# Attention in a fused transformer block: heads one after another, two K/V/q slots, and exp in pieces of 1024 columns

## The reference

```python
xn = _layernorm(x)
x = x + attn(xn, W_qkv, b_qkv, W_out, b_out) + ffn(xn, gate_w, fc1_w, ..., alpha)
# attn
att = jnp.einsum('bhqd,bhkd->bhqk', q, k) * SCALE
att = jax.nn.softmax(jnp.where(causal, att, -jnp.inf), axis=-1)
out = jnp.einsum('bhqk,bhkd->bhqd', att, v)
# ffn: softmax gate, top 2 of 8 experts, gelu(x @ fc1) @ fc2, weighted sum
```

## Time and profile before

| | |
|---|---|
| median of the two runs | 7725.79 us (7260.15 and 8191.42) |
| profiled execution | 7260.15 us, span of its slowest core 7258.6 us |
| spans of all cores | 7247.8 to 7258.6 us, granted clock 0.871 to 0.873 |
| busy over the span | PE 79%, PEld 34%, DVE 20%, ACT 12%, POOL 8% |
| attention | 1166 to 2669 us |

### The profile page before, as it was taken

One profiled execution on the slowest core, in us unless ns is written; L12 is line 12 of the kernel. 1 busy time (PEld: TensorE's weight loads), 2 busy tenths in 40 slices (PEclk: granted clock), 3 DMA queues, 4 the chain that ended last, 5 costly groups with the idle time before them and its releaser, 6 DMA issues.

```text
span 7258.6 us, 69207 instructions; the slowest of 8 cores (7247.8 to 7258.6 us)
## 1 busy us (share of the span) xinstructions
PE 5759.5 (79%) x26321; PEld 2479.1 (34%) x26321; DVE 1438.2 (20%) x2612; ACT 855.4 (12%) x1651; POOL 554.2 (8%) x697
## 2 busy tenths in 40 slices
PE   2987882555555536659999999999699999999998
PEld 1432331222222212224444444444244444444443
DVE  5011003333333320001111111112112111111111
ACT  2100012233333320000000000000000000000000
POOL 0000000000000000000111111110011101110110
PEclk9988895666666667879999999999799999999999
DMA  3532402000000023374655556464765645555563
GB/s 100 70 53 41 79 32 76 24 24 24 24 23 24 15 51 95 95 157 59 72 68 70 70 61 79 59 81 50 162 79 59 82 58 71 69 71 69 61 79 81
DMA packets 737986, 474.56 MB, mean 65 GB/s; under 512 B 671984, under 2 KB 672128, under 8 KB 727424
## 3 DMA queue, kind: packets, MB, share of 16 engines
q0 software_dynamic: 642688, 310.67, 35.2%
q1 hardware_dynamic: 86000, 125.90, 5.8%
q10 hardware_dynamic: 8976, 33.56, 1.2%
HBM read 696.81 MB, written 75.50 MB: 106 GB/s over the span
## 4 chain that ended last, share of the span: by engine, by line
PE 76%; DVE 8%; issue 6%; DMA 4%; ACT 3%; another core or an unknown queue 1%; DVEq 1%; ACTq 0%; SPq 0%
PE psB L90 40%; PE psA L90 36%; DVE st L90 2%; ACT p_sb L90 2%; DVE p_sb L90 2%; DMA ct_sb<-ctxT_d 1%; DVE pT_sb L90 1%; DMA acc_sb<-out 1%; DVE o_sb L90 1%; DVE knm_sb L90 1%; DVE cte_sb L90 0%; ACT hT_sb L90 0%; DMA out<-acc_sb 0%; DVEq L89 0%
## 5 line engine op out<-in xcount | busy, mean ns | idle before, releaser
L90 PE MATMUL psA<-xnc_sb,f_sb 128*128 128x512 bf16 x8192 | 1816.4, 380 | 124.4 <-DMA acc_sb<-out 124.4
L90 PE MATMUL psB<-f_sb,hT_sb 128*128 128x512 bf16 x8192 | 1848.7, 384 | 47.3 <-ACT hT_sb L90 47.3
L90 DVE SCALAR_TENSOR_TENSOR acc_sb<-psB,comb_sb,acc_sb 128x1024 f32<-128x1024 f32 x512 | 657.3, 1284 | 3416.8 <-PE psB L90 3416.8
L90 PEld LDWEIGHTS psA<-xnc_sb,f_sb 128*128 128x128 bf16 x8192 | 782.7, 98 | 1139.8 <-issue 232.4
L90 PEld LDWEIGHTS psB<-f_sb,hT_sb 128*128 128x128 bf16 x8192 | 788.0, 99 | 1091.9 <-issue 209.0
L90 ACT ACTIVATE hT_sb<-psA 128x1024 bf16<-128x1024 f32 x256 | 262.4, 1025 | 3692.0 <-PE psA L90 3692.0
L90 POOL DMA_DIRECT2D f_sb<-fc_w x512 | 435.2, 861 | 3139.3 <-PE psB L90 1852.0
L90 PE MATMUL psB<-ident_sb,p_sb 128*128 128x128 bf16 x2176 | 306.0, 299 | 399.1 <-DVE p_sb L90 206.0
L90 ACT ACTIVATE p_sb<-psA,bnd_sb 128x512 bf16<-128x512 f32 (+3 forms) x640 | 400.2, 625 | 1061.3 <-PE psA L90 1011.8
L90 PE MATMUL psB<-pT_sb,vh_sb 128*128 128x512 bf16 (+3 forms) x640 | 225.8, 531 | 202.0 <-DVE p_sb L90 201.3
L90 PEld LDWEIGHTS psB<-ident_sb,p_sb 128*128 128x128 bf16 x2176 | 197.5, 129 | 509.5 <-issue 509.3
(11 more groups left out here) (93 smaller groups left out, 1894.8 us busy)
## 6 DMA issues: line engine op xcount, KB each, us to landing
f_sb<-fc_w POOLq DMA_DIRECT2D x512, 512.0 KB, 11.7
xt_sb<-x SPq DMA_DIRECT2D x16, 1024.0 KB, 5.0
wqk_sb<-w_qkv POOLq DMA_DIRECT2D x32, 512.0 KB, 10.0
x_sb<-x SPq DMA_DIRECT2D x16, 1024.0 KB, 9.1
out<-o_sb SPq DMA_DIRECT2D x16, 1024.0 KB, 5.1
acc_sb<-out SPq DMA_DIRECT2D x2, 8192.0 KB, 41.0
out<-acc_sb SPq DMA_DIRECT2D x2, 8192.0 KB, 27.7
qT_d<-ev_sb ACTq DMA_DIRECT2D x16, 512.0 KB, 7.6
```

The lines of the kernel that those rows point to most:

```text
L90: instr = getattr(engine, name)(*a, **kw)
```

## The change

It alters three things in stage 3.

1. The groups of a head run one after the other: (0,0), (0,1), (0,2), (0,3), (1,0), ... The bound of head h + 1 stands at the start of (h, 2); only head 0's stands ahead of the first group.
2. K, V and q have two slots each, and so has bnd_sb; the load of head h + 1 is listed at (h, 1). The columns for row sums are shared by blocks of the same parity.
3. Scores and exp work in pieces of 1024 keys: up to two matmuls of 512 (and the mask) fill half of psA, and one ACTIVATE reads it. psA is now two buffers, ps_P0 and ps_P1.

```diff
-        groups = []
-        for hp in range(0, n_h, 2):
-            for g in range(4):
-                groups.append((hp, g))
-                if hp + 1 < n_h:
-                    groups.append((hp + 1, g))
+        groups = [(h, g) for h in range(n_h) for g in range(4)]
...
-            ksl = h % 3
-            dk = (d_kA, d_kB, d_kC)[ksl]
+            ksl = h % 2
+            dk = d_kA if ksl == 0 else d_kB
...
-            if g == 1 and h % 2 == 0 and h + 2 < n_h:
-                kv_rdys[h + 2] = plan_kv_load(h + 2)
-                q_rdys[h + 2] = plan_q_load(h + 2)
+            if g == 1 and h + 1 < n_h:
+                kv_rdys[h + 1] = plan_kv_load(h + 1)
+                q_rdys[h + 1] = plan_q_load(h + 1)
...
                 plan_bnd(0)
-                if n_h > 1:
-                    plan_bnd(1)
-            if g == 2 and h % 2 == 0 and h + 2 < n_h:
-                plan_bnd(h + 2)
+            if g == 2 and h + 1 < n_h:
+                plan_bnd(h + 1)
...
-                lidx = (gi % 2) * 2 + (qbi % 2)
-                ab = 8 + 4 * lidx
-                P.guard_wait("scalar", f"lcols{lidx}")
-                for nb in range(nbs):
-                    n0 = nb * 512
-                    n1 = min(K, n0 + 512)
-                    bk = (bank_cur + nb) % 4
-                    b0 = bk * 512
+                ab = 8 + 4 * (qbi % 2)
+                nbs2 = (K + 1023) // 1024
+                P.guard_wait("scalar", f"lcols{qbi % 2}")
+                for nb in range(nbs2):
+                    n0 = nb * 1024
+                    n1 = min(K, n0 + 1024)
+                    pk = (bank_cur + nb) % 2
+                    b0 = pk * 1024
...
-                        i = t.matmul(ps_S[:, b0:b0 + (n1 - n0)],
-                                     qg[:, qbi * 128:(qbi + 1) * 128],
-                                     kth[:, n0:n1], start=True, stop=not diag)
+                        i = None
+                        for s0 in range(n0, n1, 512):
+                            s1 = min(n1, s0 + 512)
+                            i = t.matmul(ps_S[:, b0 + s0 - n0:b0 + s1 - n0],
+                                         qg[:, qbi * 128:(qbi + 1) * 128],
+                                         kth[:, s0:s1], start=True,
+                                         stop=not (diag and s1 == n1))
...
-                    P.set_guard(f"ps_S{bk}", se, se.n)
-                bank_cur = (bank_cur + nbs) % 4
+                    P.set_guard(f"ps_P{pk}", se, se.n)
+                bank_cur = (bank_cur + nbs2) % 2
...
-                    for nb in range(1, nbs):
+                    for nb in range(1, nbs2):
...
-            if g == 3 and h % 2 == 1 and h + 2 < n_h:
-                kv_rdys[h + 2] = plan_kv_load(h + 2)
-                q_rdys[h + 2] = plan_q_load(h + 2)
-                plan_bnd(h + 2)
```

More of the change, by code:

```diff
@@ L161, in build @@
         d_kB = Sem(ctx, nc, "d_kB")
-        d_kC = Sem(ctx, nc, "d_kC")
-        d_qC = Sem(ctx, nc, "d_qC")
         d_qA = Sem(ctx, nc, "d_qA")
@@ L598, in build @@
         a3 = ExitStack()
-        kt_sb = a3.enter_context(nc.sbuf_tensor("kt_sb", [128, 3 * S], BF16))
-        vh_sb = a3.enter_context(nc.sbuf_tensor("vh_sb", [128, 3 * S], BF16))
-        qh_sb = a3.enter_context(nc.sbuf_tensor("qh_sb", [128, 3 * S], BF16))
+        kt_sb = a3.enter_context(nc.sbuf_tensor("kt_sb", [128, 2 * S], BF16))
+        vh_sb = a3.enter_context(nc.sbuf_tensor("vh_sb", [128, 2 * S], BF16))
+        qh_sb = a3.enter_context(nc.sbuf_tensor("qh_sb", [128, 2 * S], BF16))
         p_sb = a3.enter_context(nc.sbuf_tensor("p_sb", [128, 8 * S], BF16))
@@ L604, in build @@
         cte_sb = a3.enter_context(nc.sbuf_tensor("cte_sb", [128, 2 * 512], BF16))
-        st3 = a3.enter_context(nc.sbuf_tensor("st3", [128, 28], F32))
+        st3 = a3.enter_context(nc.sbuf_tensor("st3", [128, 16], F32))
         q2_sb = a3.enter_context(nc.sbuf_tensor("q2_sb", [128, S], BF16))
-        bnd_sb = a3.enter_context(nc.sbuf_tensor("bnd_sb", [128, 4 * NT], F32))
+        bnd_sb = a3.enter_context(nc.sbuf_tensor("bnd_sb", [128, 2 * NT], F32))
         ps_S = psA
@@ L633, in plan_kv_load @@
         def plan_kv_load(h):
-            ksl = h % 3
-            dk = (d_kA, d_kB, d_kC)[ksl]
+            ksl = h % 2
+            dk = d_kA if ksl == 0 else d_kB
             kth = kt_sb[:, ksl * S:(ksl + 1) * S]
             vh = vh_sb[:, ksl * S:(ksl + 1) * S]
-            P.guard_wait("sync", f"kvh{ksl}")
+            P.guard_wait("sync", f"kv{ksl}")
             def s_kv(sy, h=h, kth=kth, vh=vh, dk=dk):
@@ L650, in plan_q_load @@
         def plan_q_load(hq):
-            qsl = hq % 3
-            dq = (d_qA, d_qB, d_qC)[qsl]
+            qsl = hq % 2
+            dq = d_qA if qsl == 0 else d_qB
             qh = qh_sb[:, qsl * S:(qsl + 1) * S]
-            P.guard_wait("sync", f"qh{qsl}")
+            P.guard_wait("sync", f"q{qsl}")
             def s_q(sy, hq=hq, qh=qh, dq=dq):
@@ L662, in plan_bnd @@
         def plan_bnd(hh):
[L663 to L666, removed]
+            hpar = hh % 2
+            dqh = d_qA if hpar == 0 else d_qB
+            qhf = qh_sb[:, hpar * S:(hpar + 1) * S]
             P.wait("vector", dqh, q_rdys[hh])
@@ L674, in plan_bnd @@
             P.wait("tensor", ve, q2_ve)
-            P.guard_wait("tensor", "ps_S0")
+            P.guard_wait("tensor", "ps_P0")
             def t_qn(t):
@@ L695, in plan_bnd @@
             bnd_ve = ve.n
-            P.set_guard("ps_S0", ve, bnd_ve)
+            P.set_guard("ps_P0", ve, bnd_ve)
             P.wait("scalar", ve, bnd_ve)
@@ L707, in build @@
             par = gi % 2
-            ksl = h % 3
-            dk = (d_kA, d_kB, d_kC)[ksl]
+            ksl = h % 2
+            dk = d_kA if ksl == 0 else d_kB
             vh = vh_sb[:, ksl * S:(ksl + 1) * S]
             kth = kt_sb[:, ksl * S:(ksl + 1) * S]
-            if g == 1 and h % 2 == 0 and h + 2 < n_h:
-                kv_rdys[h + 2] = plan_kv_load(h + 2)
-                q_rdys[h + 2] = plan_q_load(h + 2)
+            if g == 1 and h + 1 < n_h:
+                kv_rdys[h + 1] = plan_kv_load(h + 1)
+                q_rdys[h + 1] = plan_q_load(h + 1)
             kv_rdy = kv_rdys[h]
             q_rdy = q_rdys[h]
-            qsl = h % 3
-            dq = (d_qA, d_qB, d_qC)[qsl]
+            qsl = h % 2
+            dq = d_qA if qsl == 0 else d_qB
             qg = qh_sb[:, qsl * S + g * 512:qsl * S + (g + 1) * 512]
@@ L739, in build @@
                 P.wait("tensor", dk, kv_rdy)
[L741 to L748 removed]
+                ab = 8 + 4 * (qbi % 2)
[6 more added lines that the diff above has]
+                    b0 = pk * 1024
                     diag = (n1 == K)
[L750 removed]
+                    P.guard_wait("tensor", f"ps_P{pk}")
                     def t_s(t, qbi=qbi, qb=qb, n0=n0, n1=n1, b0=b0, qg=qg,
                             kth=kth, diag=diag):
[L754 to L756 removed]
+                        i = None
[5 more added lines that the diff above has]
+                                         stop=not (diag and s1 == n1))
                         if diag:
@@ L771, in sc_exp @@
                                           AF.Exp,
-                                          bias=bnd_sb[:, (h % 4) * NT + qb:
-                                                      (h % 4) * NT + qb + 1],
+                                          bias=bnd_sb[:, (h % 2) * NT + qb:
+                                                      (h % 2) * NT + qb + 1],
                                           scale=SCALE,
@@ L776, in build, with v_li, v_ps2 @@
                     P.on("scalar", sc_exp)
-                    P.set_guard(f"ps_S{bk}", se, se.n)
-                bank_cur = (bank_cur + nbs) % 4
+                    P.set_guard(f"ps_P{pk}", se, se.n)
+                bank_cur = (bank_cur + nbs2) % 2
+                if qbi == 3:
+                    P.set_guard(f"q{qsl}", pe, pe.n)
                 exp_se = se.n
                 if qbi == 3 and g == 3:
-                    P.set_guard(f"bndbuf{h % 4}", se, exp_se)
+                    P.set_guard(f"bndbuf{h % 2}", se, exp_se)
                 P.wait("vector", se, exp_se)
-                def v_li(vv, nbs=nbs, ab=ab, lidx=lidx):
+                def v_li(vv, nbs2=nbs2, ab=ab, qbi=qbi):
                     a = st3[:, ab:ab + 1]
-                    for nb in range(1, nbs):
+                    for nb in range(1, nbs2):
                         vv.tensor_add(a, a, st3[:, ab + nb:ab + nb + 1])
-                    i = vv.reciprocal(st3[:, 2 + lidx:3 + lidx], a)
+                    i = vv.reciprocal(st3[:, 2 + qbi % 2:3 + qbi % 2], a)
                 P.on("vector", v_li)
-                P.set_guard(f"lcols{lidx}", ve, ve.n)
+                P.set_guard(f"lcols{qbi % 2}", ve, ve.n)
                 P.wait("vector", ve, ve.n)
-                def v_ps2(vv, pq=pq, K=K, lidx=lidx):
+                def v_ps2(vv, pq=pq, K=K, qbi=qbi):
                     i = vv.tensor_scalar(pq[:, 0:K], pq[:, 0:K],
```

(4 more changed lines are left out.)

5 lines of the change are left out of this document (removed).

## The result

| | before | changed |
|---|---|---|
| median of all runs | 7581.59 us (13 runs) | 7428.57 us (14 runs) |
| lowest | 7259.7 us | 7135.42 us |
| ratio | | 0.9852, 95% interval 0.9806 to 0.9899 |
| core 0: span | 7258.0 us | 7125.5 us |

The changed kernel is 1.5% faster (1.0 to 1.9%), 124 us between the lowest runs; within 2%, as the likeliest case had it. The medians lie some 300 us above the lowest runs because in many executions of both kernels the cores of one or both dies show a lower granted clock for part of the time, so all that follows compares lowest runs, and of the traces the stretch of attention on cores where it was not so. From lowest to lowest run the ratio is 0.983; the 0.9852 also counts a run of 7202.51. The rows of the changed kernel are those of core 0.

What follows compares the result with a forecast made beforehand. It took attention to be bound by a circle of waits between TensorE, ScalarE and VectorE, with no engine full. Its terms, -3 - 5 - 107 = -115 us, taken from the profiled 7260, gave 7145 us, range 7080 to 7215.

Steps and rivals of the forecast that it cites:

- the likeliest case: Whole kernel: a measured time within 2% of the kernel before, chance 0.81.
- term 1: Attention, new order of groups: -0.41 us per head pair, -3 us in all.
- term 2: Start of attention: first scores wait for one bound, -6.9 us; head 1's bound costs 1.76 later; net -5 us.
- term 3: Attention, exp in pieces of 1024 columns: 6.7 us less per head, -107 us over 16 heads.
- The bound's credit: Attention groups holding a bound computation: it costs 1.76 us each, credited twice per head pair.
- rival A: Attention: TensorE's clock rises with shorter waits, -60 us more, 7085 us; chance 0.12.
- A stall from having two halves: Block 3 of g = 2 groups: exp waits about 0.1 us because only two PSUM buffers are left.
- rival B: Attention exp: a joining saves only 0.19 us on ScalarE, 48 us less gained, 7193 us; chance 0.07.
- At no cost: Loads of K, V and q with two slots add no time; without cover, up to 7 us a head.
- C: Attention: the order is not neutral, bounds hide less than credited, +25 us for term 1, 7173 us; chance 0.08.
- D: Attention: coarser hand-overs keep TensorE at 1.2 GHz, 184 to 361 us more, 7329 to 7506 us; chance 0.04.

Runs made afterwards that it cites:

- x9: Changed kernel with pieces of 512, four banks and four sets of sums put back, leaving the new order, two slots and later bound: 7232.14 us at the lowest.
- x3: Changed kernel with the removed row-sum adds put back as adds of a zero column: 7206.48 us.
- x4: Kernel before with exp that accumulates no row sum, the adds kept: 7200.37 us and 7200.74 us, ratio 0.9926.
- x2: Kernel before with only pieces of 1024, two PSUM halves and fewer row-sum adds: 7155.21 us, ratio 0.9886.

## Why the prediction was right or wrong

The mechanism was right in outline: the stage is a circle of waits, the wide exp brings most of the gain, and the stage lost what the sum had for it and some 12 us more. The stated time was not: the median over all runs is 7428.57 us, outside 7080 to 7215.

The step that failed is the base of the sum, "the trace is of the first and I forecast against it". 7145 is 115 us less than the one profiled execution, 7260.15. The median of the kernel before, over 13 runs, is 7581.59, and the changed kernel's lies 153 us below it. The median given already stood 466 us above the profiled run; I noted the distance without putting it into the range, and a forecast of a median over such executions had to reach up to them. Against the three lowest runs 7145 compares with 7135 to 7141 us.

Part of that closeness is luck, since two terms are off in opposite directions. "Measured" in this table is in means over the cores, for the sums of groups 1473.6 us before, 1452.0 in x9 and 1352.9 in the changed kernel.

| | predicted | measured |
|---|---|---|
| term 1, order of groups | -3 | -23 |
| term 2, start | -6.9, and +1.8 for the bound that moves | -6.6, and +1.7 |
| term 3, wide exp | -107 | -99 |
| sum, and time | -115, 7145 | -127 (attention), 7135 |

The lowest runs differ by 124 us; the rest is within what the cores differ by.

**Term 1: mis-sized, 3 for 23.** Taking the groups' durations from the kernel before assumed that a kind costs the same whatever stands two groups ahead. The bound's credit held (1.7 us). With the new order TensorE stays longer at its upper level, and the 63 groups became 22 us shorter where my sum had them 1 to 2 us shorter (-3, and 1.8 for the bound that moves in). This is rival A's mechanism at somewhat over a third of its size and in a place that I had not named: not shorter waits but other neighbours. The granted clock over the groups shows it, small as it is: 0.61 to 0.62 on the eight cores before, 0.64 on the eight of x9.

**Term 2: right.** From the first bound to the first score matmul 5.9 to 7.0 us were saved, 6.6 in the mean. That the first score matmul of core 0 is only 4.7 us earlier lies in the start of the first bound, which varies by several us from core to core.

**Term 3: right in size, not in its parts.** With x9 as its base, (1 after 0) lost 1.0 (I had 1.3), (2 after 1) 1.4 (1.4) and (3 after 2) 3.9 us (4.0). I had given 53 us to ScalarE and 54 to VectorE. With the adds kept, ScalarE's part is 30, and the adds then bring 71. That the two errors cancel is luck. For ScalarE I had 0.25, 0.6 and 2.5 us a group at g = 1, 2 and 3, and x3 against x9 shows none, 0.1 and 1.8. On the adds the step that failed is that block 2's are hidden: x3 shows all 16 adds of a head paid for. A stall from having two halves could only be at block 3 of g = 2; there the next ACTIVATE starts 0.31 us behind the READ_ACCUMULATOR's start, against 0.29 in the row of the g = 3 group above (1557.47 to 1557.76), so 0.02 us instead of 0.1 (core 0):

```profile
1547.36 0.58 ACT L90 ACTIVATE p_sb<-psA,bnd_sb 128x384 bf16<-128x384 f32 x1
1547.84 0.19 ACT L90 ACTIVATION_READ_ACCUMULATOR p_sb<-psA,bnd_sb 128x1 f32 x1
1548.15 1.11 ACT L90 ACTIVATE p_sb<-psA,bnd_sb 128x1024 bf16<-128x1024 f32 x1
```

The 0.44 a joining held, as the pitch of 1.30 us shows, but not the reason given for its excess over the 0.19 of rival B. I laid all of it to the READ_ACCUMULATOR; x4 shows 0.09 us for that, and most of the rest is that neighbours do not overlap in this program.

**At no cost: held.** VectorE waited for a q load once, at the start. No load is on the path.

**Rivals.** B (7193) falls by x2 and by the pitch of 1.30 us. C (the order costs) has the wrong sign. D (TensorE stays at 1.2 GHz, a granted clock of 0.50) falls: the stage was granted 0.63. Its lower end was added up wrongly, half of 361 us is 180 and not 184. A is the one that was partly true.

## What to carry to other kernels

When the profile shows all engines half idle and waiting for each other in a ring, nearly every small instruction in the ring counts at its full start-to-start distance (here with a wait of the plan in front of each). With the exps joined, taking out 256 adds of one column was worth 71 us; joining 256 exps while the adds stayed was worth 30. But ask first which wait closes the ring: a wait on "everything listed so far" cost 180 us here, and listing the next block's scores ahead of the last group's leftovers another 220, against 124 for the whole change. When two gains act on engines that take turns in ending last, do not book them separately. And before forecasting a median, look at how far the median of the old kernel lies from the run that was profiled.

## What the runs showed of the hardware

The order of equal work changes TensorE's level: the same seven transposes took 0.91 or 0.55 us by what stood before them. Inside one trace a group with the same instructions took 23.68 us at a granted clock of 0.64 and 24.83 at 0.51. An accumulated exp of 512 columns, each started after the one before it is done, costs 0.87 us from start to start, 0.78 without the accumulator; one of 1024 columns costs 1.30. A row-sum add of one column costs 0.26 us in such a chain, of which 0.16 are shown as busy.
